# TensorE's opening and wide-chunk loop placed in a branch inside a two-turn loop

## What is computed

```python
def _layernorm(x, axis=-1, eps=1e-05):
    m = jnp.mean(x, axis=axis, keepdims=True)
    v = jnp.var(x, axis=axis, keepdims=True)
    return (x - m) / jnp.sqrt(v + eps)
...
def reference(x, adj, L0_gnn_u):
    def _L0_gnn_ref(x, adj, u):
        P_DROP = 0.1
        keep = (u >= P_DROP).astype(x.dtype)
        x_drop = x * keep / (1.0 - P_DROP)
        return jnp.matmul(adj, x_drop)
    x = _layernorm(x + _L0_gnn_ref(x, adj, L0_gnn_u), axis=-1)
    return x
```

## Time and profile before

| | us |
|---|---|
| median of 3 runs (641.74 to 641.94) | 641.75 |
| the profiled execution, its own time | 641.88 |
| its span, from first to last instruction | 640.1 |
| TensorE busy with matmuls | 502.8 |
| VectorE busy | 53.7 |
| ScalarE busy | 17.7 |

### The profile page before, as it was taken

How to read it: one execution, slowest core, us unless ns; L and a number is a source line. 1 busy time by engine, 2 the same in 40 slices (tenths; PEclk the granted TensorE clock), 3 DMA queues, 4 the chain that set the end, 5 groups by cost and what they waited for, 6 DMA issues and landing times.

```text
span 640.1 us, 5097 instructions
## 1 busy us (share of the span) xinstructions
PE 502.8 (79%) x2312; PEld 179.7 (28%) x2312; DVE 53.7 (8%) x102; ACT 17.7 (3%) x41; POOL 1.6 (0%) x14
## 2 busy tenths in 40 slices
PE   0097969688799578879878689867869868689997
PEld 0062213232233222223222223222323223133344
DVE  1930001010010100101000010100101001010101
ACT  0001000000000000000000000000000000000000
POOL 1000000000000000000000000000000000000000
PEclk9997979988799978889979899978999969799999
DMA  9999999999999999999999999999999999999998
GB/s 393 459 394 455 431 420 454 405 446 439 422 421 436 435 451 422 438 408 444 459 418 434 442 412 455 420 434 446 426 418 426 446 451 422 438 405 438 425 425 364
DMA packets 7207, 274.84 MB, mean 429 GB/s; under 512 B 800, under 2 KB 928, under 8 KB 1312
## 3 DMA queue, kind: packets, MB, share of 16 engines
q1 hardware_dynamic: 7056, 272.63, 98.8%
q10 hardware_dynamic: 144, 2.10, 0.8%
HBM read 272.63 MB, written 2.10 MB: 429 GB/s over the span
## 4 chain that ended last, share of the span: by engine, by line
DMA 62%; PE 33%; DVE 3%; another core or an unknown queue 1%; issue 0%; ACT 0%; SPq 0%; DVEq 0%; ACTq 0%
DMA ring<-adj 56%; PE acc L202 33%; DMA ring<-adj_last 5%; DMA xdrop<-u 2%; DVE node_sum L317 1%; DVE xdrop L321 1%; DVE xdrop L329 1%; PE folded L210 0%; DVE x_sb L321 0%; PE lifted L237 0%; SPq L126 0%; ACT squares L303 0%; PE lifted L263 0%; ACT std L308 0%
## 5 line engine op out<-in xcount | busy, mean ns | idle before, releaser
L202 PE MATMUL acc<-ring,xdrop 128*64 128x512 f32 (+1 forms) x2176 | 485.6, 606 | 103.1 <-DMA ring<-adj 101.7
L202 PEld LDWEIGHTS acc<-ring,xdrop 128*64 128x64 f32 x2176 | 162.8, 146 | 413.0 <-issue 280.2
L344 DVE SCALAR_TENSOR_TENSOR y<-folded,x_sb 128x256 f32<-128x256 f32 (+1 forms) x16 | 6.7, 416 | 552.3 <-PE folded L210 552.3
L237 PE MATMUL lifted<-x_sb,lift 128*128 128x64 f32 x4 | 1.1, 428 | 30.6 <-DVE x_sb L321 30.6
L210 PEld LDWEIGHTS folded<-fold,sums_T 128*128 128x128 f32 x128 | 15.5, 191 | 12.6 <-issue 12.6
L284 ACT COPY sums_T<-acc 128x512 f32<-128x512 f32 x15 | 8.8, 585 | 335.0 <-PE acc L202 335.0
L210 PE MATMUL folded<-fold,sums_T 128*128 128x64 f32 x128 | 17.7, 281 | 0.0
L277 ACT ACTIVATE std<-square_sum,eps 128x4 f32<-128x4 f32 (+1 forms) x16 | 4.8, 297 | 225.2 <-DVE square_sum L351 225.2
L237 PEld LDWEIGHTS lifted<-x_sb,lift 128*128 128x128 f32 x4 | 0.9, 322 | 30.5 <-issue 30.5
L348 DVE TENSOR_TENSOR squares<-y 128x256 f32<-128x256 f32 (+1 forms) x16 | 6.7, 417 | 0.5
L355 DVE TENSOR_TENSOR x_sb<-y,rstd 128x256 f32 (+1 forms) x16 | 6.7, 416 | 0.6
(11 more groups left out here) (23 smaller groups left out, 5.5 us busy)
## 6 DMA issues: line engine op xcount, KB each, us to landing
ring<-adj SPq DMA_DIRECT2D x13, 4096.0 KB, 31.3
ring<-adj SPq DMA_DIRECT2D x2, 2048.0 KB, 28.7
xdrop<-u ACTq DMA_DIRECT2D x1, 2048.0 KB, 12.5
x_sb<-x SPq DMA_DIRECT2D x1, 2048.0 KB, 12.3
out<-x_sb SPq DMA_DIRECT2D x1, 1984.0 KB, 12.7
ring<-adj_last SPq DMA_DIRECT2D x1, 1920.0 KB, 29.5
ring<-adj_last SPq DMA_DIRECT2D x1, 1792.0 KB, 33.4
ring<-adj_last SPq DMA_DIRECT2D x1, 1536.0 KB, 30.6
```

Source lines behind the costliest of these rows:

```text
L202: last = nc.tensor.matmul(acc[i][D * h:D * h + D, 0:cols], xdrop[:, k, :], piece[:, b, :], start=(k < 2), stop=(k >= NB - 2))
L344: nc.vector.scalar_tensor_tensor(out=y[:, 0:nj, :], in0=folded[:, 0:nj, :], scalar=1.0 / KEEP, in1=x_sb[:, bass.ds(block0, nj), :], op0=AL ...
```

## The change

TensorE's program is put into a loop of two turns, L257, with a branch inside it, L258. On the first turn the branch's condition is false, and TensorE's sequencer goes from the compare-and-branch straight to the instruction behind the branch's body. On the second turn the body runs: the opening and the whole loop over wide chunks. The tail stands behind the two-turn loop, as before it stood behind the chunk loop. The opening and the body of the chunk loop are now the functions `opening` and `wide_chunk`, with the same instructions in the same order. No other engine's program is touched.

```diff
-            pe.wait_ge(lift_ready, 1)
...
-            with pe.Fori(0, (CHUNKS - 1) // RING) as f:
-                for v, i in enumerate(ACC_OF):
-                    for n in range(HALVES):
-                        half(i, f, v * HALVES + n)
-                        if n == 0:
-                            fold_rows(f * RING + v)
+            def opening():
+
+                pe.wait_ge(lift_ready, 1)
+                pe.wait_ge(x_centred, 1)
+                for j in range(LAST_J):
+                    nc.tensor.matmul(lifted[:, j, 0:D], lift[:, :], x_sb[:, NB - LAST_J + j, :],
+                                     start=True, stop=False)
+                pe.wait_ge(fold_ready, 1)
+
+                pe.wait_ge(row_in[0], 16)
+                for n in range(HALVES):
+                    pe.wait_ge(dropped, n + 1)
+                    first = first_narrow + n * HALF
+                    last = products(1, narrow[:, first:first + HALF, :], n * HALF, HALF, LAST_COLS)
+                    if n % 2:
+                        last.then_inc(half_used, 1)
+
+            def wide_chunk(f, v):
+                for n in range(HALVES):
+                    half(ACC_OF[v], f, v * HALVES + n)
+                    if n == 0:
+                        fold_rows(f * RING + v)
+
+
+            with pe.Fori(0, 2) as turn:
+                with pe.If(turn > 0):
+                    opening()
+
+                    with pe.Fori(0, (CHUNKS - 1) // RING) as f:
+                        for v in range(RING):
+                            wide_chunk(f, v)
```

## The result

| | median us | runs | ratio to before, 95% interval |
|---|---|---|---|
| before | 641.75 (641.65 to 642.08) | 18 | |
| changed | 643.0 (642.79 to 643.57) | 18 | 1.002 (1.0013 to 1.0026) |

The changed kernel is 1.25 us slower, 0.2%. Its profiled execution took 643.03 us with a span of 641.2 us, 1.15 us more than before's 641.88.

The account below looks back on a forecast made before the run. DMA engines that never rest were taken as the bound, level with TensorE in the last 30 us; 641.88 + 0 + 0 + 0 = 641.9 us, with the runs' median 0.13 us below, gives 641.8; range 641.2 to 643.0 us.

Parts of the forecast that it names:

- point 3 of the change: TensorE's code fetches: the jump brings packets early, so none for the loop's end in the first pass; on the path 0.
- none between 180 and 215 us: Sign of being right: no instruction packet in that stretch, near the end of the chunk loop's first pass.
- the third term of the sum: Early code packets delaying x, u and the opening: 0 on the path, +2.0 us with the covers gone.
- its two covers: After the opening: TensorE sits 3.52 us until a load lands; SyncE issues the next load some 10 us ahead.
- landings of the parts later by 1 us: Sign of being wrong: loads of the parts near the end land 1 us later.
- rival A: Jump displaces code on the core: one doubled packet 642.8, tail stall 643.4, both 644.4 us; chance 0.12, one doubling alone 0.05.
- Point 1: Added sequencer instructions at the start, 0.83 and 0.28 us at most, while TensorE waits for VectorE: on the path 0.
- Point 2: Way out of the branch ahead of the tail: 0.52 us at most under 4.4 us of cover, on the path 0.
- The estimate of the stall: First turn's jump to code not yet there: sequencer waits 1 to 3 us, bounds 1.0 and 12.5 us.
- B: First turn's fetches delay the opening beyond its cover; needs some 40 us of them to cost; far end 0.01.
- C: Earlier packets relieve the late engine of the last landings: up to 1.0 us faster, 640.8 us; chance 0.04.
- D: Branch brings no code early: seven packets at the old times, 641.8 us; chance 0.84 together with forecast and B.

Follow-up runs that it names:

- e1_near: Changed kernel with the two-turn loop and branch around the opening alone, chunk loop and tail following as before: 641.85 us, ratio 1.0.
- e3_pad512: Kernel before with 1024 already satisfied waits (512 idle instructions) added ahead of the opening, no branch: 660.92 us, ratio 1.0299.
- e6_skip5x512: Kernel before with five jumps in a row at the start of TensorE's program, each over 512 idle instructions: 645.79 us, ratio 1.0067.
- e7_short_before: Kernel before with 56 of the opening's 64 products left out, TensorE's code 224 instructions shorter: 641.82 us, ratio 1.0.
- e4_turns3: Changed kernel with three turns instead of two, two of them passing over the branch's body: 643.14 us, ratio 1.0019.
- e11_skip2x256: Kernel before with two jumps at the start of TensorE's program, each over 256 idle instructions: 643.05 us, ratio 1.0018.
- e2_pad256: Kernel before with 512 already satisfied waits (256 idle instructions) added ahead of the opening, no branch: 641.87 us, ratio 1.0001.

## Why the prediction was wrong

The forecast was 641.8 us, no change; the result is 643.0, slower by 1.25 us and at the very end of the range, which was drawn so as to take in one doubled packet.

**The step that failed is the last of point 3 of the change**, "In exchange the packets of the end of the loop should no longer come in the first pass". They came: two between 180 and 216 us, with two more at the start. The count was nine and not seven. That code already fetched would not be fetched again I took from the later passes of the loop, where this holds. For the code that the jump brought early it did not hold by the count of packets, and the row that could have warned me was missing: before had no jump to code that was not yet there.

With it failed the third term of the sum, "On the path: 0" for the early packets. It followed them only as far as u and the opening, where its two covers did hold. It did not follow the DMA engines that carry them, which stay behind to the end; there nine packets cost 1.19 us at the last landing. Of the prediction's own signs, "none between 180 and 215 us" failed and "landings of the parts later by 1 us" came true.

**The price of a packet was nearly right, its rule was not known.** I had it that one packet makes one engine, and so every load, late by 1.0 us, and that a second packet on the same engine costs again: rival A, "one such doubling gives 642.8". Measured were 1.5 us for an engine, 1.19 us at the part's landing and 1.25 us in the time. What failed is its weight, 0.05. The prediction had no rule for the engine to which a packet goes, and I thought it unlikely that a few more would meet on one; with sixteen engines nine packets need not. They use eight. With seven packets before, one more was free and the second was not. The landings of single DMA engines in the trace of before, 627.23 and later for seven of them, were there to be read; but with nine undisturbed engines beside them they could not show the limit of eight.

**What held.** Point 1, the control flow at no cost: e1_near, 641.85 us. Point 2, the way out of the branch with 4.4 us of cover: in the changed kernel TensorE's gap before the tail is 0.42 us, as before. Of point 3, the early packets delay u by 1.4 us (2.0 at the worst was allowed) and the covers take it: e1_near, with u 1.5 us late and the whole opening, 641.85 us. The estimate of the stall was 1 to 3 us and the measured value 5.7; the bounds of 1.0 and 12.5 held, and no harm came of it, since it ends at 6.7 us. The loop's branch back took 0.22 and 0.23 us (0.22 and 0.24 before), and there were no packets between 216 and 624 us.

**The weighing against the Trainium skill.** In the Trainium skill, "Runtime: NRT & Kernel Launch", section "Instruction fetch mechanics", says that a taken branch beyond the two-page window forces a fetch. For the first far jump the trace agrees (5.7 us). For the same jump a second time it does not: 0.23 us in the run with three turns. The prediction's "that is eight" was its own division of the figures in "Advanced Engine Details and Errata", section "ISA Cache"; that section of the Trainium skill also says "Only 2 cache lines!", which the loop's branches back without a packet do not bear out for TensorE.

**Rivals.** A happened in its mild form; the stall at the tail did not. B did not happen in the changed kernel, but e3_pad512 shows its mechanism at full price, 19 us, and its bound of 10 us was too wide: in e6_skip5x512 the second wide load was issued 7.9 us later than before, and the undisturbed engines had already lost 1.8 us. C did not happen, and e7_short_before shows that even one packet less brings nothing: others remain, as C's text had it. D is excluded by the two packets of the first 15 us.

## What to carry to other kernels

Where the DMA engines never rest, a load is as late as its most disturbed engine: look at the sixteen landings of one load, not only at the last, and count the instruction packets beside them. As long as TensorE's stalls stay under their cover, adding code, or a jump over more than a block of it, was free here up to eight packets, the number of engines that carry code. The ninth cost 1.2 to 1.4 us wherever the early packets were, and twelve cost little more; a second step beyond sixteen was not cleanly seen. In the changed kernel 224 instructions less took the 1.2 us away, though these were products that the result needs. Fewer packets brought nothing: six cost what eight do, and in the trace of before the spread of a load's landings is 1.9 us with one late engine and 1.8 us with seven. No version faster than the kernel before came out of this; one without any packet under the loads was not tried.

## What the runs showed of the hardware

- Instruction packets went to eight of the sixteen DMA engines in turn, as the landings tell it. In no run up to 17 packets were more than eight engines late.
- A packet of 16 KB holds its engine for 1.0 us and makes it 1.5 us late; a second one moves the last landing by 1.2 to 1.5 us (changed kernel 1.19, e4_turns3 1.49). Two packets that are under way at once hold their engines for 1.8 us each and make them about 3 us late.
- A TensorE jump to code that is not on the core stalled the sequencer for 5.3 (e11_skip2x256) to 9.5 us (e6_skip5x512) with loads under way; to code that is there it took 0.2 to 0.4 us (0.36 us into the next block in e1_near's first jump, 0.23 for a far one in e4_turns3).
- Code fetched by a jump is there for a second jump 1 us later, yet packets for the same number of blocks come again in the first pass. What gives way to what stays open, and so does which eight engines carry code.
- An idle wait instruction on TensorE's sequencer shows 51 ns and takes 106 ns from one to the next (e2_pad256, e3_pad512).
